# Macaron block on one Trainium2 core: where the transposes of the second gated layer stand, which wait follows the moved first pair, and when the first norm's rows are made

## The reference

```
def _L0_ffn_ref(x, We, be, Wg, bg):          # 8 experts, the best 2 of each row
    gates = softmax(x_flat @ Wg + bg)
    topk_gates, topk_idx = top_k(gates, 2);  topk_gates = topk_gates / sum(topk_gates)
    expert_out = einsum('nd,edo->neo', x_flat, We) + be
    out = sum(take_along_axis(expert_out, topk_idx) * topk_gates)

def _L0_attn_ref(x, ...):                    # 16 heads of 16, three neighbours
    xp = x @ Wp.T + bp;  q, k, v = projections of xp
    kn, vn = k and v of the rows i-1, i, i+1 (cyclic in the 2048 rows of a batch)
    attn = softmax(einsum('bshd,bsnhd->bshn', q, kn))
    return einsum(attn, vn) @ Wo.T + bo

x = x + 0.5 * ffn(layernorm(x));  x = x + attn(layernorm(x));  x = x + 0.5 * ffn(layernorm(x))
```

## Time and profile before

| | before |
|---|---|
| median of 3 runs | 1111.66 us (1111.09 to 1112.69) |
| the profiled execution | 1111.69 us |
| its span, first to last instruction | 1109.8 us |
| PE busy | 1053.9 us (95%) |
| DVE busy | 889.9 us (80%) |
| POOL busy | 719.9 us (65%) |
| ACT busy | 529.1 us (48%) |
| TensorE clock granted, mean | 0.984 of full speed |

### The profile page before, as it was taken

How to read it: one execution, slowest core, us unless ns; L and a number is a source line. 1 busy time by engine, 2 the same in 40 slices (tenths; PEclk the granted TensorE clock), 3 DMA queues, 4 the chain that set the end, 5 groups by cost and what they waited for, 6 DMA issues and landing times.

```text
span 1109.8 us, 17795 instructions
## 1 busy us (share of the span) xinstructions
PE 1053.9 (95%) x5459; PEld 882.1 (79%) x5459; DVE 889.9 (80%) x2441; ACT 529.1 (48%) x1181; POOL 719.9 (65%) x953
## 2 busy tenths in 40 slices
PE   5898799999999999999999999999999999999885
PEld 3677688888888888888888888888888888887663
DVE  3658688888889888888888888888888888888783
ACT  3254455454555554445554454455554545544331
POOL 2476476666777666677777666777766667665353
PEclk9899899999999999999999999999999999999998
DMA  5001000000000000000000000000000000000000
GB/s 166 10 30 36 12 15 6 19 20 21 19 20 20 11 10 20 20 20 20 21 20 1 20 20 20 20 20 20 16 6 20 20 20 20 11 10 1 20 10 19
DMA packets 12582, 23.04 MB, mean 21 GB/s; under 512 B 2212, under 2 KB 5812, under 8 KB 12488
## 3 DMA queue, kind: packets, MB, share of 16 engines
q1 hardware_dynamic: 9240, 13.37, 3.4%
q0 software_dynamic: 3248, 8.54, 2.8%
HBM read 12.47 MB, written 8.39 MB: 19 GB/s over the span
## 4 chain that ended last, share of the span: by engine, by line
PE 77%; DVE 6%; POOL 5%; issue 4%; SPq 3%; DMA 2%; ACT 2%; POOLq 0%; DVEq 0%; ACTq 0%
PE ffn_bank L887 17%; PE ffn_bank L888 17%; PE ffn_bank L889 17%; PE tr_bank L916 5%; PE tr_bank L928 4%; PE mix_bank L889 4%; PE mix_bank L888 4%; PE mix_bank L887 4%; SPq L250 2%; POOL base L331 2%; PE tr_bank L887 1%; PE tr_bank L888 1%; PE tr_bank L889 1%; DMA we_raw<-in_L_ffn_We 1%; POOL rstd L319 1%
## 5 line engine op out<-in xcount | busy, mean ns | idle before, releaser
L887 PE MATMUL ffn_bank<-we_hi,T_hi 128*128 128x512 f32 x1024 | 415.0, 405 | 3.5 <-DVE chain_sum L658 3.0
L889 PE MATMUL ffn_bank<-we_hi,T_lo 128*128 128x512 f32 x1024 | 403.1, 394 | 0.0
L888 PE MATMUL ffn_bank<-we_lo,T_hi 128*128 128x512 f32 x1024 | 401.8, 392 | 0.0
L453 ACT ACTIVATE we_raw<-ffn_bank,gate 128x256 f32<-128x256 f32 x512 | 208.6, 474 | 140.3 <-PE ffn_bank L889 138.8
L339 POOL TENSOR_TENSOR chain_sum<-chain_sum,we_raw 128x512 f32<-128x512 f32 x128 | 165.9, 1296 | 130.4 <-DVE chain_sum L658 129.1
L887 PEld LDWEIGHTS ffn_bank<-we_hi,T_hi 128*128 128x128 f32 x1024 | 194.3, 190 | 42.4 <-DVE chain_sum L658 4.6
L889 PEld LDWEIGHTS ffn_bank<-we_hi,T_lo 128*128 128x128 f32 x1024 | 193.7, 189 | 43.0
L888 PEld LDWEIGHTS ffn_bank<-we_lo,T_hi 128*128 128x128 f32 x1024 | 194.6, 190 | 34.5
L416 ACT CAST T_hi<-tr_bank 128x512 fp32r<-128x512 f32 x128 | 75.0, 588 | 168.1 <-PE tr_bank L916 167.9
L658 DVE SCALAR_TENSOR_TENSOR chain_sum<-ffn_bank,gate,chain_sum 128x256 f32<-128x256 f32 x256 | 111.7, 478 | 44.3 <-PE ffn_bank L889 43.6
L316 POOL TENSOR_TENSOR var_eps<-mean_var,eps 128x2 f32<-128x2 f32 x96 | 28.9, 301 | 136.9 <-DVE mean_var L576 136.9
(11 more groups left out here) (125 smaller groups left out, 1818.0 us busy)
## 6 DMA issues: line engine op xcount, KB each, us to landing
out_x<-y SPq DMA_DIRECT2D x31, 256.0 KB, 2.0
we_raw<-in_L_ffn_We SPq DMA_DIRECT2D x2, 1024.0 KB, 14.0
x_in<-in_L_attn_x,x_row POOLq DMA_INDIRECT x60, 3.1
x_in<-in_L_attn_x SPq DMA_DIRECT2D x2, 256.0 KB, 7.4
moved_qk<-qk SPq DMA_DIRECT2D x4, 124.0 KB
w_raw<-in_L_attn_Wq SPq DMA_DIRECT2D x1, 256.0 KB, 2.9
w_raw<-in_L_attn_Wk SPq DMA_DIRECT2D x1, 256.0 KB, 3.1
w_raw<-in_L_attn_Wv SPq DMA_DIRECT2D x1, 256.0 KB, 3.8
```

The source lines that it names most:

```text
L453: last = nc.scalar.activation(scaled[:, f, t, half, j], ffn_bank[b][:, j * D:(j + 1) * D], ACT.Copy, scale=gate[:, 2 * f + t, e:e + 1])
L887: nc.tensor.matmul(dest, hi[:, t, k, :], w_hi_[:, k, c0:c1], start=(first and k == 0), stop=False, skip_group_check=not first)
L888: nc.tensor.matmul(dest, hi[:, t, k, :], w_lo_[:, k, c0:c1], start=False, stop=False, skip_group_check=not first)
L889: last = nc.tensor.matmul(dest, lo[:, t, k, :], w_hi_[:, k, c0:c1], start=False, stop=(k == KB - 1), skip_group_check=not first)
```

## The change

Three edits. (1) In steps 4 to 30 PE does TD(s-3) after all four banks of FFN2 tile 1 and directly ahead of TB(s), eight transposes in a row; accordingly ACT copies TD's high part after the scaling of FFN2 tile 1, and DVE makes the low part after its chain. From step 31 on the old places stay; below step 4 there is no FFN2 and only the places on ACT and DVE move. (2) Each of the three moved buffers has its own semaphore of 8 transfers, and each of the three waiting parts waits for its own alone. (3) ACT normalises LN1's rows of pair s+2 in step s, between LN3's rows and the exponential, and no longer as the first part of step s+1.

```
-MOVES = 3 * 2 * B
+MOVES = 2 * B
 # semaphores
-        pair_moved = sem("pair_moved")
+        qk_moved, v_moved, x1_bo_moved = sem("qk_moved"), sem("v_moved"), sem("x1_bo_moved")
 # SP, step 1: same transfers, same order
-                                         source[...]).then_inc(pair_moved, 16)
+                                         source[...]).then_inc(arrived, 16)
 # POOL x1_bo_step / ACT qk_step / ACT v_step, for pairs 2 and 32
-                    pool.wait_ge(pair_moved, 16 * MOVES)
+                    pool.wait_ge(x1_bo_moved, 16 * MOVES)
-                    act.wait_ge(pair_moved, 16 * MOVES)
+                    act.wait_ge(qk_moved, 16 * MOVES)
-                    act.wait_ge(pair_moved, 16 * MOVES)
+                    act.wait_ge(v_moved, 16 * MOVES)
 # ACT body
+                drains = s.reg is None and s.const >= PAIRS - 1
-                if s.const >= 0 and (s + 1).within(PAIRS):
-                    normalise_step(LN1, s + 1)
                 if ffn1:
                     scale_step(FFN1, s, 0)
...
                     normalise_step(LN3, s - 3)
-                if (s - 3).within(GROUPS):
+                if (s - 3).within(GROUPS) and drains:
                     hi_step(TD, s - 3)
+                if (s + 2).within(PAIRS):
+                    normalise_step(LN1, s + 2)
                 if (s - 2).within(GROUPS):
                     exp_step(s - 2)
                 if ffn2:
                     scale_step(FFN2, s - 4, 1)
+                if (s - 3).within(GROUPS) and not drains:
+                    hi_step(TD, s - 3)
                 if ffn1 and not filling:
                     hi_step(TB, s)
 # DVE body
-                if (s - 3).within(GROUPS):
+                if (s - 3).within(GROUPS) and drains:
                     lo_step(TD, s - 3)
...
                     chain_step(FFN2, s - 4, 1, 3)
+                if (s - 3).within(GROUPS) and not drains:
+                    lo_step(TD, s - 3)
                 if ffn1 and not filling:
                     lo_step(TB, s)
 # PE body
-                    ffn_step(FFN2, s - 4, s, 1, range(0, 2 if drained else 1))
+                    ffn_step(FFN2, s - 4, s, 1, range(0, 2 if drained else 1 if drains else 4))
                 if (s - 3).within(GROUPS):
                     T_step(TD, s - 3, s)
-                if (s - 4).within(GROUPS):
+                if (s - 4).within(GROUPS) and drains:
                     ffn_step(FFN2, s - 4, s, 1, range(2 if drained else 1, 4))
                 if s.within(PAIRS) and not filling:
                     T_step(TB, s, s)
```

More of the change, by code:

```diff
@@ L241, in body @@
                 if s.reg is None and s.const == 1:
-                    for moved, source, done, value in ((moved_qk[:], qk[:, 0:2], qk_copied, 2),
-                                                       (moved_v[:], v[:, 0:2], v_copied, 1),
-                                                       (moved_x1_bo[:], x1_bo[:, 0:2], x1_bo_done, 1)):
+                    for moved, source, done, value, arrived in (
+                            (moved_qk[:], qk[:, 0:2], qk_copied, 2, qk_moved),
+                            (moved_v[:], v[:, 0:2], v_copied, 1, v_moved),
+                            (moved_x1_bo[:], x1_bo[:, 0:2], x1_bo_done, 1, x1_bo_moved)):
                         sp.wait_ge(done, value)
@@ L248, in body @@
                             sp.dma_start(moved[ROWS * b:ROWS * (b + 1) - 1],
-                                         source[ROWS * b + 1:ROWS * (b + 1)]).then_inc(pair_moved, 16)
+                                         source[ROWS * b + 1:ROWS * (b + 1)]).then_inc(arrived, 16)
                             sp.dma_start(moved[ROWS * (b + 1) - 1:ROWS * (b + 1)],
-                                         source[ROWS * b:ROWS * b + 1]).then_inc(pair_moved, 16)
+                                         source[ROWS * b:ROWS * b + 1]).then_inc(arrived, 16)
                 a = s - 4
```

## The result

The changed kernel takes 1097.03 us (median of 4 runs, 1096.75 to 1098.24), the kernel before beside it 1112.02 us. The ratio is 0.9866, with a 95% interval of 0.9851 to 0.9881: 15.0 us or 1.3% less, clear of the 0.2% that a measurement can tell. The profiled execution took 1097.25 us with a span of 1095.2 us, so its span is 14.6 us shorter than that of before.

The account below looks back on a forecast made before the run. PE's own work and short stops, chiefly TD's, were taken to bound the steady stretch. Savings of 6.3 + 2.2 + 4.0 + 1.7 = 14.2 us took 1111.7 to 1097.5 us; 8-in-10 range 1094 to 1104 us.

Parts of the forecast that it names:

- Part 1: Joined transposes in steps 4 to 30: TD's stop for LN3's rows goes, saving 6.3 us.
- Nothing is late next: Steady steps: with TD's low part made later, TA does not wait and FFN1's next bank has 1.0 us to spare.
- Part 2, steady: LN1's rows ahead of the exponential on ACT in steady steps: cost nothing, covered by 0.32 us and the bank's 1.0 us.
- Part 2, filling: Earlier LN1 rows from step 2 to 3: attention transposes of step 3 start sooner, 2.2 us kept.
- Part 3: Semaphore per buffer in step 3: the Q/K copy's DMA wait goes, 4.0 us, and half clock behind it, 1.7 us.
- Step 3's last stop: PE's 3.69 us stop at TD of group 0 stays, as does the 6.8 us of half clock behind it.
- rival A: Third slow stretch, at TD in step 3, shrinks as well: up to 2.3 us more, 1095.2 us; chance 0.14.
- B: Steady steps: another wait takes the place of TD's, joined transposes bring nothing, 1103.8 us; chance 0.14.
- F: Whole kernel: the change does not do what it says, 1111 us; chance 0.02.
- C: Filling: slow clock stretches stay behind shorter stops, 1.7 us at 115 and about 1.7 behind step 2, 1100.9 us; chance 0.12.
- D: Step 3: DMA counts complete late, costing 5.7 us, 1103.2 us; chance 0.03.
- E: Steady steps slower: POOL's late shift makes LN1's rows hold up exponential and scaling, from 1.3 us lateness; chance 0.05.

Follow-up runs that it names:

- late_apart: The changed kernel with TD standing alone between banks 1 and 2 of FFN2 tile 1, not joined with TB; 1097.48 us.
- changed_again: The changed kernel's unedited code measured once more on one chip; 1097.02 us.
- ln1_thrice: The changed kernel with four more activations of LN1's size, results unused, ahead of LN1's rows in 26 steps; 1111.63 us.
- join_sem: The changed kernel with LN1's rows back at the start of the next step; 1097.72 us.
- join_sem_again: Repeat, on one chip with the changed kernel, of that kernel with LN1's rows back at the start of the next step; 1098.52 us.
- sem_only: The kernel before with only a semaphore per moved buffer added; 1105.50 us.
- ln1_only: The kernel before with only LN1's rows made in the step before, between TD's copy and the exponential; 1111.97 us.
- join_ln1: The changed kernel with one semaphore for all moved buffers again; 1105.30 us.
- join_only: The kernel before with only the joined transposes and TD's two copies in their new places; 1104.81 us.

## Why the prediction was right, point by point

**Bound.** This was right. PE bounded the steady stretch but for one stop a step, and that stop was TD waiting for LN3's rows. late_apart shows it.

**Part 1.** Said 6.3 us, of it 4.3 in the even and 2.0 in the odd steps. The trace gives 6.8 us over the steady steps, 0.36 us in each even one and 0.15 in each odd one; the four pairs of medians in the table that differ in this edit alone give 6.7 to 7.8 us. The step's reading was right, the term about 0.5 us small. Other traces with the joined transposes have 885.2 to 885.8 us between the marks where this one has 885.3. In changed_again, which has 885.7, the difference is spread evenly, 31.66 against 31.64 us in each step, so that there the saving is 6.3 us. I can't say what these 0.02 us a step are. "Nothing is late next" held: DVE has a new wait for POOL, which costs PE nothing.

**Part 2, steady.** It was costed at nothing, under a cover of 0.32 us at the exponential and 1.0 us at the bank. That was right: 0.26 us were left at the exponential. Of the 1.98 us that ln1_thrice adds (four times 0.495), an even step pays 0.83 and an odd one 0.26 us, so the cover is 1.15 us in the even and 1.72 us in the odd steps, where 1.3 was said for both.

**Part 2, filling.** Said 2.2 us. Between the marks it is 2.3 us with all three edits, but this is a comparison with an execution of before that had the slow stretch; against kernels that differ in this edit alone it is 0.7 to 1.5 us by the medians and 0.9 us by the marks of join_sem and join_sem_again. The times of the steps were close (98.53 for the transposes is 43.66 behind the second gate transpose; said were 96.95 - 53.29 = 43.66). What was mis-sized is the part of the gain that came from the clock, about 1.3 us, which I took to be there in each execution.

**Part 3.** Said 4.0 + 1.7 = 5.7 us; the marks show 4.1 and 1.7 us in the changed kernel and in sem_only alike. The median of sem_only is 6.6 us down; the 0.9 us more are not in these marks, and open. A side estimate was off without harm: V was put at 109.5, and starts at 109.68 - 1.58 = 108.1 us if the longer setup is taken off. `x1_bo_step` did not wait for its transfers in either trace. The rule of the Trainium skill, "DMA: Bandwidth & Descriptors", section "Queues, rings and completion order", is that completion is not in order of issue for one issuing engine. It cost nothing here: of 24 transfers on SP's queue the 8 of `qk` had all landed by 108.56 us, when its copy started without a wait for them, with 0.15 MB of that queue still to come by 114 us. Whether the 8 transfers of one buffer land in order among themselves no trace shows. What I hadn't seen is that part 2 depends on part 3. The sum adds both edits, for which it holds, but the 2.2 us stood there as if part 2 alone would bring them; ln1_only and join_ln1 show 0.

**Step 3's last stop and rival A.** The stop of 3.69 us stayed to the hundredth. The slow stretch at it was 3.4 us long in the profiled execution and not 6.8, which gave 1.1 us of the 2.3 us of rival A; in changed_again it was 6.8, and 0.3 us were left of the gain (5.70 us from TD to the TA and TB block, against 4.83 here and 5.97 before). Rival A is thus no other outcome, but something that some executions have, and its price was about double what a trace shows. The new wait of TA for TD's copy did not show.

**Rivals B to F.** B fell: no other wait took TD's place. C fell: the stretch at 115 us is absent in each trace with the split semaphore, and the one behind step 2 in each trace with LN1's rows moved. D fell with sem_only, and F with the result. E: the shift was in time; its mechanism is real, as ln1_thrice shows, but its decision point of 1.3 us of lateness is not reached.

**The sum.** 14.2 us said; 14.6 us in the profiled execution, made of 6.80 + 2.34 + 4.13 + 1.67 + 1.14 + 0.1 at the end, less 1.58 us of a slow stretch in the setup. That the total hit within 0.5 us is in part luck: +0.5 and +1.1 us against -1.6 us.

## What to carry to other kernels

Where PE is busy throughout, look at its starts and not at its busy time: here a stop of 0.3 us a step was hidden in modelled durations, and the cure was to put 4 us of other work ahead of the waiting instruction. An edit that brings an engine sooner to a wait with a fixed end, such as a DMA that lands at the same time anyway, is worth nothing until that wait is gone; price it together with the edit that removes the wait. Price added instructions from start to start, and give the cover that hides them a number before they are moved. If steps alternate, read an even and an odd one before multiplying.

## What the runs showed of the hardware

A stop of TensorE of 2.27 us in step 2 was followed by some 3.4 us at half clock in three traces (before, join_only, sem_only) and not in two others (join_sem, join_sem_again); sem_only and these two have the same code up to there. The stops of 0.94 us that stand in its place in the other traces were never followed by one. The stop of 3.69 us was met by half clock in each trace that has it, for 3.4 us or for 6.8; in the changed kernel it was 3.4 us in one execution and 6.8 in another. There the longer one began at 117.5 us, while PE still stood (until 119.03).

What 3.4 us at half clock cost differs with what PE has to do in it: 1.6 us in the setup (the first row of the table of marks), 1.3 us behind step 2 (53.79 against 52.48 us), 1.5 us in the draining (TO of group 29 to the next TO, 24.94 us in changed_again against 23.40), 0.9 us for the second half of the long one in step 3 (5.70 against 4.83 us). One at 56 us cost nothing: from the second gate transpose to TO of step 3 the changed kernel took 51.53 us with it and 51.55 us, in changed_again, without. That such stretches are most of the scatter of some 3 us between the runs of one kernel is likely and not shown. Of 39 runs of the kernel before, the 17 with the lowest mean clock (0.981) took 1112.07 to 1113.76 us and the three with the highest (0.987) 1110.92 to 1111.05 us, but one at 0.986 took 1113.32 us.

Going from matmuls to transposes and back cost nothing measurable: four transposes took 0.44 us alone, and eight in a row 0.88 us.
